# Layer-0 routed feed-forward: weights kept in SBUF for both stages, the sorted token list made by one-hot products, rows gathered and the residual added slot by slot

## The chip, the cores and the metric

The kernel runs on one core of a Trainium2 chip. The metric is device time in microseconds (us) of one launch: the median of several runs for a comparison, and one profiled execution for the reading of the trace. Engines are called by the profile's names: PE (TensorE), DVE (VectorE), ACT (ScalarE), POOL (GpSimd) and SP (SyncE, which only issues transfers).

## The reference, cut to what matters

Twelve stages run one after another on 4096 tokens of 128 numbers (16 x 256). The change concerns the routed feed-forward of layer 0, which runs twice, before and after the layer's attention. Each time the tokens are normalised, sent to one of 8 experts by the largest router logit, and the expert's output is added to the token.

```python
# x: 4096 tokens of DIM = 128, already layer-normed; HIDDEN = 512, E = 8
logits = jnp.einsum('bsd,de->bse', x, router_w) + router_b
top1 = jnp.argmax(jax.nn.softmax(logits, axis=-1), axis=-1)
out = jnp.zeros_like(x)
for i in range(E):
    h = jnp.einsum('bsd,df->bsf', x, w1[i]) + b1[i]          # 128 -> 1024
    a, g = jnp.split(h, 2, axis=-1)
    y = jnp.einsum('bsh,hd->bsd', a * jax.nn.sigmoid(g), w2[i]) + b2[i]
    out = out + jnp.where((top1 == i)[..., None], y, 0.0)
```

## The kernel before, in words

A stage is a block in which each engine has its own instruction stream, written out by hand; engines meet only at semaphores, and at a barrier between stages. `STAGES` lists them: `l0_ffn`, `l0_attn`, `l0_ffn`, and then three stages for each of the layers 1 to 3.

`l0_ffn` has four phases.

1. **Normalise and route.** Eight chunks of four tiles (128 tokens each). DVE writes `xn` (`ln_dve`, L178), PE turns it (L188), ACT keeps it (L194), PE multiplies by the router's weights (L561), DVE adds the bias (L401). POOL makes the scales `rstd` (L159) and copies each chunk of `xn` to `sent` (L368). In the same time SP loads all the stage's weights (L326 to L332: `w1` 4 MB, `w2` 2 MB, the biases spread over the partitions 4.5 MB) and, behind them, writes zeros over the sorted table in DRAM (L337).
2. **Place.** DVE finds each token's row in a list sorted by expert, in which every expert begins on a multiple of 128 (L411 to L469, `pos_i` and `owner_i`). POOL scatters the 32 tiles of normalised rows with their token numbers to `sorted_dram` (L377, 32 indirect transfers); when all have landed, SP loads the table back to `sent` (L342).
3. **Slots.** 40 slots of 128 sorted rows, each with one expert. Per slot: ACT fills `xs` (L515), PE turns it (L580), ACT keeps `xst` (L519), PE makes the two halves `hg` and `ha` (L586, L587), DVE adds the bias (L476, L477), ACT takes the sigmoid (L523), DVE multiplies (L481), PE turns four blocks (L611), ACT keeps `ht` (L547), PE multiplies by `w2` (L594), DVE adds `b2` into `pad` (L486), POOL scatters the result by token number to `sums_dram` (L384). The streams run some slots apart (`run_slots`: body `i` has the first steps of slots `i+1` to `i+3` beside the last ones of `i-1`), and a hardware loop holds two bodies.
4. **Add back.** When all scatters have landed, SP loads `sums_dram` in four pieces (L346), DVE adds each chunk to `x` and takes the new statistics (L505, L201).

## Time and profile before

| | us |
|---|---|
| median of 3 runs | 3355.55 (3349.03 to 3359.73) |
| profiled execution, its own time | 3350.59 |
| span in its trace | 3348.9 |
| PE busy | 2403.8 (72%) |
| DVE busy | 1590.5 (47%) |
| ACT busy | 1083.1 (32%) |
| POOL busy | 849.2 (25%) |
| mean granted TensorE clock | 0.837 of 2.4 GHz |

The span runs from the first to the last instruction; 1.7 us lie around it. The stages follow each other in time, so a stage's own stretch tells what it is worth, and a mean over the span does not. The first `l0_ffn` runs from 13.43 to 271.50 us of the span, the second from 439.40 to 700.79 us. A row of the timeline gives the start, the duration of the merged instructions, engine, line, operation, what is written and read, the count, and in brackets the idle time before it with what ended it.

### The profile page before, as it was taken

What the parts mean: (1) busy time and instruction counts of PE and PEld (TensorE: products, weight loads), DVE (VectorE), ACT (ScalarE), POOL (GpSimd) and SP (SyncE); (2) the same over time, 40 slices, a digit from 0 to 9 for tenths busy, and PEclk for the clock granted to TensorE, in tenths of its full rate; (3) what the DMA queues carried; (4) which work ended last, traced back from release to release, by engine and by line L of the source; (5) the groups of instructions that cost most, each with busy time, mean ns of one, the idle gap of its engine ahead of it and who ended that gap; (6) DMA issues with size and microseconds to landing.
All of it is one profiled execution on the core that took longest, in us unless ns stands there. A gap on an engine that the chain in (4) does not pass through costs nothing. (4 is left out here: it accounts for less than half of the span.)

```text
span 3348.9 us, 45143 instructions
## 1 busy us (share of the span) xinstructions
PE 2403.8 (72%) x13128; PEld 1597.5 (48%) x13129; DVE 1590.5 (47%) x3638; ACT 1083.1 (32%) x2400; POOL 849.2 (25%) x759
## 2 busy tenths in 40 slices
PE   2696945953647361098799971495999879889998
PEld 2463533633635360087466650494444435544554
DVE  3466943675257527933333349634111267761110
ACT  1342312422223121064344431263222135563222
POOL 4323433223611361077100010384000112200000
PEclk9997957985578555599899985697999878999999
DMA  7101062033522356066200013265000043310000
GB/s 202 54 20 30 1 171 59 19 97 84 113 56 77 81 109 182 1 132 136 58 1 1 1 38 92 52 144 138 0 0 0 19 100 78 83 43 26 0 0 25
DMA packets 316644, 211.22 MB, mean 63 GB/s; under 512 B 64711, under 2 KB 300171, under 8 KB 313963
## 3 DMA queue, kind: packets, MB, share of 16 engines
q1 hardware_dynamic: 282731, 177.16, 19.5%
q0 software_dynamic: 33792, 32.57, 5.9%
q8 instruction: 61, 1.00, 0.1%
q14 instruction: 60, 0.49, 0.0%
HBM read 147.94 MB, written 61.12 MB: 62 GB/s over the span
## 5 line engine op out<-in xcount | busy, mean ns | idle before, releaser
L159 POOL TENSOR_TENSOR rstd<-ln_t,power 128x4 f32<-128x4 f32 (+1 forms) x96 | 96.9, 1021 | 636.3 <-DVE ln_t L152 635.9
L2286 DVE TENSOR_TENSOR x<-x,s_y 128x512 f32 (+1 forms) x16 | 11.0, 688 | 496.8 <-PE s_y L2365 496.8
L2350 PE MATMUL s_z<-s_ha,s_wt_h 128*128 128x512 f32 x512 | 222.4, 592 | 0.0
L2357 PE MATMUL s_z<-s_hb,s_wt_h 128*128 128x512 f32 x512 | 222.3, 592 | 0.0
L1897 PE MATMUL s_hu<-s_xgt,s_w 128*128 128x128 f32 x768 | 195.3, 399 | 1.7 <-ACT s_xgt L1837 0.9
L2576 DVE TENSOR_REDUCE s_mx<-s_sa 128x2 f32<-128x512 f32 x256 | 167.1, 685 | 61.3 <-PE s_sa L2729 59.9
L2657 ACT ACTIVATE s_e<-s_sc 128x512 f32<-128x512 f32 x256 | 149.6, 599 | 123.9 <-PE s_sc L2745 122.4
L1897 PEld LDWEIGHTS s_hu<-s_xgt,s_w 128*128 128x128 f32 x768 | 186.7, 327 | 3.0 <-issue 3.0
L188 PE MATMUL s_tp<-ident,xn 128*128 128x128 f32 x352 | 71.5, 339 | 152.1 <-DVE xn L178 148.1
L1883 PE MATMUL s_lp<-ident,s_posf 48*128 48x48 f32 x2 | 0.6, 312 | 233.6 <-DVE s_prob L1765 233.6
L1706 POOL DMA_INDIRECT s_xg<-rows_dram,s_from_i x96 | 95.8, 998 | 269.2 <-DVE s_to_i L1769 240.5
L1718 POOL DMA_INDIRECT acc_dram<-s_yo,s_to_i x96 | 153.4, 1598 | 41.5 <-issue 28.7
L2357 PEld LDWEIGHTS s_z<-s_hb,s_wt_h 128*128 128x128 f32 x512 | 97.3, 190 | 122.5 <-issue 122.5
L2350 PEld LDWEIGHTS s_z<-s_ha,s_wt_h 128*128 128x128 f32 x512 | 96.2, 190 | 115.8 <-issue 115.8
L2729 PE MATMUL s_sa<-s_kx,s_qx 72*128 72x256 bf16 x512 | 112.4, 306 | 36.3 <-DVE s_mx L2576 20.8
L188 PEld LDWEIGHTS s_tp<-ident,xn 128*128 128x128 f32 x352 | 51.1, 175 | 181.7 <-DVE xn L178 137.6
L476 DVE TENSOR_TENSOR s_gb<-s_hg,s_b 128x512 f32<-128x512 f32 x80 | 55.3, 692 | 172.7 <-PE s_ha L587 172.6
L384 POOL DMA_INDIRECT sums_dram<-s_pad,s_sent x80 | 77.7, 972 | 224.7 <-DVE s_pad L486 224.7
L178 DVE TENSOR_SCALAR xn<-x,mean,rstd 128x128 f32 (+1 forms) x352 | 113.5, 424 | 29.0 <-POOL rstd L159 15.4
L194 ACT ACTIVATE xnt<-s_tp 128x512 f32<-128x512 f32 x88 | 52.5, 597 | 210.0 <-PE s_tp L188 202.3
L1102 POOL DMA_INDIRECT acc_dram<-s_yo,s_to_i x64 | 101.5, 1586 | 61.9 <-DMA acc_dram<-s_yo,s_to_i 49.5
L2341 PE MATMUL s_z<-xnt,s_wt_w 128*128 128x512 f32 x256 | 112.7, 593 | 4.6 <-ACT s_wt_w L2300 4.6
(406 smaller groups left out, 5687.6 us busy)
## 6 DMA issues: line engine op xcount, KB each, us to landing
s_w<-in_L_ffn_W_dram SPq DMA_DIRECT2D x96, 256.0 KB
s_kx<-k_dram SPq DMA_DIRECT2D x16, 576.0 KB
s_qx<-q_dram SPq DMA_DIRECT2D x48, 192.0 KB
s_w<-in_L_ffn_w_dram SPq DMA_DIRECT2D x2, 4096.0 KB, 14.4
s_b<-in_L_ffn_b_dram SPq DMA_DIRECT2D x16, 512.0 KB, 7.1
acc_dram<-s_zero SPq DMA_DIRECT2D x16, 512.0 KB, 6.2
acc_dram<-x SPq DMA_DIRECT2D x4, 2048.0 KB, 9.7
x<-acc_dram SPq DMA_DIRECT2D x16, 512.0 KB, 7.0
```

Of the source, the lines that this page charges most:

```text
L159: pool.tensor_tensor(core.rstd[:, tiles], core.ln_t[:, 2, tiles], core.power[:, 0:CT], ALU.pow).then_inc(s.scale_ready.sem, 1)
L178: last = dve.tensor_scalar(core.xn[:, u, j, :], core.x[:, bass.ds(t, 1), :], core.mean[:, bass.ds(t, 1)], core.rstd[:, bass.ds(t, 1)], ALU ...
L188: last = pe.transpose(s.tp[:, u % s.tp_banks, j * P:(j + 1) * P], core.xn[:, u, j, :], core.ident[:, :])
L1102: pool.indirect_dma_start(sums, bass.IndirectOffsetOnAxis(ap=to_i[:, n:n + 1], axis=0), yo[:, n % RING, :], None, compute_op=ALU.add).then ...
L1718: pool.indirect_dma_start(sums, bass.IndirectOffsetOnAxis(ap=to_i[:, n:n + 1], axis=0), yo[:, n % RING, :], None, compute_op=ALU.add).then ...
L1897: last = pe.matmul(hu[:, u, j * P:(j + 1) * P], w1[:, q, :, :].rearrange("p s m -> p (s m)")[:, j::S], xgt[:, u, :], start=True, stop=True)
L2341: pe.matmul(z[:, (2 * f + half) % 4, :], wt[m][:, 0, f * P:(f + 1) * P], core.xnt[:, u, :], start=True, stop=True).then_inc(group_done.sem, 1)
L2350: last = pe.matmul(z[:, o, :], wt["h1"][:, f, o * P:(o + 1) * P], ha[:, f, :], start=f == 0, stop=f == HB - 1)
L2357: last = pe.matmul(z[:, o, :], wt["h2"][:, f, o * P:(o + 1) * P], hb[:, f, :], start=f == 0, stop=f == HB - 1)
L2576: dve.tensor_reduce(mx[:, i, t, 2 * pairs:2 * pairs + 2], sa[:, n % 2, :, :], AX.X, ALU.max).then_inc(max_done.sem, 1)
L2657: act.activation(e[:, n % RING, :, :], sc[:, n % 2, :, :], ACT.Exp).then_inc(exp_done.sem, 1)
L2729: last = pe.matmul(sa[:, n % 2, a, :], qx[0:ROWS, slot, h, t * P:(t + 1) * P], kx[0:ROWS, slot, h, :], start=True, stop=True)
```

## The change

What it does, by part:

- **Weights kept.** `L0Weights` holds router, `w1`, `b1`, `w2`, `b2` and constants over the two `l0_ffn` stages and the attention between them; only the first call loads them. `w2` isn't halved any more: the 0.5 goes into the copy of `ht`. `b2` comes as three bf16 parts in three rows, and one bf16 product per slot adds it on PE.
- **Fields.** `x` becomes part of a row of 136 numbers: the token, its 6 statistics, its scale and its shift. One transfer stores all rows to `x_dram`.
- **List.** Instead of scattering rows, DVE makes one-hot matrices of a token's lane and slot, and 32 small bf16 products on PE sum the token numbers into `ids` (and `to_ids` for the way back). 39 slots take the place of 40.
- **Gather.** For each slot POOL gathers 128 rows of 544 bytes from `x_dram` into `xg`, four slots ahead of the slot whose result it then waits for. ACT normalises while it fills `xs` (scale and bias from the row).
- **Residual and statistics per slot.** DVE adds the result to the row in `xg`, after the next slot's product takes its statistics, and POOL scatters the whole row to `y_dram`. The last phase is one load of `fields` and nothing on DVE.
- The wait for the product of both halves (`h_done`) is split: `g_done` and `g_biased` for the half that the sigmoid needs. The loops of the first phase are written out.

The diff, cut to its core:

```diff
-        self.x = sb("x", [P, TILES, D])
+        self.fields = sb("fields", [P, TILES, D + 8])
+        self.x = self.fields[:, :, 0:D]
+        self.sums = self.fields[:, :, D:D + 6]
+        self.rstd = self.fields[:, :, D + 6]
...
+            sp.wait_ge(nmr_ready.sem, nmr_ready.past(0))
+            sp.dma_start(x_dram[1:TOKENS + 1, :].rearrange("(p t) d -> p t d", p=P), core.fields[:, :, :]).then_inc(x_stored.sem, 16)
...
+            ln_scales_pool(pool, core, s, range(2, CHUNKS))
+            pool.wait_ge(x_stored.sem, 32 if load else 16)
+            pool.wait_ge(ids_ready.sem, 1)
+
+            def gather(i):
+                if i >= 2:
+                    pool.wait_ge(gathered[i % 2].sem, 16 * (i // 2))
+                pool.indirect_dma_start(xg[:, i, :], None, x_dram,
+                                        bass.IndirectOffsetOnAxis(ap=ids[:, i:i + 1], axis=0)).then_inc(gathered[i % 2].sem, 16)
+
+            for i in range(4):
+                gather(i)
+            pool.wait_ge(to_ready.sem, 1)
             for i in range(SLOTS):
+                if i + 4 < SLOTS:
+                    gather(i + 4)
                 pool.wait_ge(y_kept.sem, y_kept.past(i))
...
+                pool.indirect_dma_start(y_dram, bass.IndirectOffsetOnAxis(ap=to_ids[:, i:i + 1], axis=0),
+                                        xg[:, i, :], None).then_inc(stored.sem, 16)
...
+            dve.tensor_tensor(slot_hot[:, :, :], parts[:, 0, :].unsqueeze(2).to_broadcast([P, TILES, SLOTS]),
+                              held.count[:, 0:SLOTS].unsqueeze(1).to_broadcast([P, TILES, SLOTS]),
+                              ALU.is_equal).then_inc(slots_hot.sem, 1)
+            dve.drain()
+            dve.tensor_tensor(slot_id[:, :, 1, :], slot_hot[:, :, :],
+                              held.after[:, :].unsqueeze(2).to_broadcast([P, TILES, SLOTS]), ALU.mult).then_inc(tile_ids.sem, 1)
+            for t in range(TILES):
+                last = dve.tensor_scalar(lane[:, t, :], held.count[:, :], parts[:, 1, t:t + 1], None, ALU.is_equal)
+                if t % CT == CT - 1:
+                    last.then_inc(lane_ready.sem, 1)
+            dve.wait_ge(listed.sem, 1)
+            dve.tensor_copy(id_part[:, :], ha[:, 1, 0:SLOTS])
+            dve.drain()
+            dve.scalar_tensor_tensor(ids[:, :], id_part[:, :], float(TILES), ha[:, 1, SLOTS:2 * SLOTS],
+                                     ALU.mult, ALU.add).then_inc(ids_ready.sem, 1)
...
+                dve.wait_ge(g_done.sem, g_done.past(i))
+                dve.tensor_tensor(gb[:, u, :], hg[:, u, :], b1[:, bass.ds(e, 1), HID:WIDE], ALU.add).then_inc(g_biased.sem, 1)
                 dve.wait_ge(h_done.sem, h_done.past(i))
-                dve.tensor_tensor(gb[:, u, :], hg[:, u, :], b1[:, bass.ds(e, 1), HID:WIDE], ALU.add)
                 dve.tensor_tensor(ab[:, u, :], ha[:, u, :], b1[:, bass.ds(e, 1), 0:HID], ALU.add).then_inc(biased.sem, 1)
...
-            def keep(i):
-                e = dve.value_load(owner_i[0:1, bass.ds(i, 1)], min_val=0, max_val=EXPERTS - 1)
+            def add(i):
                 dve.wait_ge(y_done.sem, y_done.past(i))
-                dve.tensor_tensor(pad[:, bass.ds(i, 1), 0:D], yp[:, 0:P], b2[:, bass.ds(e, 1), :], ALU.add).then_inc(y_kept.sem, 1)
+                xi = xg[:, bass.ds(i, 1), 0:D]
+                dve.tensor_tensor(xi, yp[:, 0:P].unsqueeze(1), xi, ALU.add).then_inc(y_taken.sem, 1)
+
+            def sums(i):
+                dve.drain()
+                dve.bn_stats(xg[:, bass.ds(i, 1), D:D + 6], xg[:, bass.ds(i, 1), 0:D]).then_inc(y_kept.sem, 1)
...
-                    keep(i - 1)
+                    add(i - 1)
                 if after:
                     gate(i + 1, 1 - u)
+                if before:
+                    sums(i - 1)
...
+            def fill_xs(i, u, half, more):
+                act.wait_ge(gathered[u].sem, half * 16 + 16 * (more + 1))
                 act.wait_ge(xt_done.sem, xt_done.past(i - 2))
-                act.activation(xs[:, u, :], sent[:, bass.ds(i, 1), 0:D], ACT.Copy).then_inc(xs_ready.sem, 1)
...
+                act.wait_ge(g_biased.sem, g_biased.past(i))
...
+            for t in range(TILES):
+                if t % CT == 0:
+                    pe.wait_ge(lane_ready.sem, lane_ready.past(t // CT))
+                last = pe.matmul(ha[:, 1, 0:2 * SLOTS], lane[:, t, :], slot_id[:, t, :, :].rearrange("p a n -> p (a n)"),
+                                 start=t == 0, stop=t == TILES - 1)
+            last.then_inc(listed.sem, 1)
...
+                pe.matmul(yp[:, 0:P], held.ones_b[:, :], b2[:, bass.ds(e, 1), :], start=True, stop=False)
                 for f in range(HB):
-                    last = pe.matmul(yp[:, 0:P], ht[:, u, f, :], w2[:, bass.ds(e, 1), f, :], start=f == 0, stop=f == HB - 1)
+                    last = pe.matmul(yp[:, 0:P], ht[:, u, f, :], w2[:, bass.ds(e, 1), f, :], start=False, stop=f == HB - 1)
...
+        with stage(nc) as kept:
+            held = L0Weights(core, kept)
+            l0_ffn(core, held, True)
+            l0_attn(core)
+            l0_ffn(core, held, False)
```

Where the change moves work, the streams are shown as the compiled programs have them (names with `s2_` or `s3_` are the first `l0_ffn`'s; `pool_dma0` is `stored`, `pool_dma1` and `pool_dma2` are `gathered`). POOL's stream from the placing to the end of the first `l0_ffn`, before:

```order
L377 DMA sorted_dram<-s_sent,s_pos_i 5120x129 [waits s2_copied,s2_pos_ready,s2_rows_zeroed]
L377 DMA sorted_dram<-s_sent,s_pos_i 5120x129 x31
L384 DMA sums_dram<-s_pad,s_sent 9216x128 [waits s2_y_kept,s2_sorted_loaded1,s2_sorted_loaded0]
L384 DMA sums_dram<-s_pad,s_sent 9216x128 [waits s2_y_kept] x39
L85 UNCONDITIONAL_BRANCH [waits pool_dma0,pool_dma1]
```

and the same place with the change:

```order
L414 DMA s_xg<-x_dram,s_ids 128x136 [waits pool_dma1]
L414 DMA s_xg<-x_dram,s_ids 128x136 [waits pool_dma2]
L414 DMA s_xg<-x_dram,s_ids 128x136 [waits pool_dma1,s3_to_ready]
L424 DMA y_dram<-s_xg,s_to_ids 9089x136 [waits s3_y_kept]
L414 DMA s_xg<-x_dram,s_ids 128x136 [waits pool_dma2]
L424 DMA y_dram<-s_xg,s_to_ids 9089x136 [waits s3_y_kept]
L414 DMA s_xg<-x_dram,s_ids 128x136 [waits pool_dma1]
L424 DMA y_dram<-s_xg,s_to_ids 9089x136 [waits s3_y_kept]
L414 DMA s_xg<-x_dram,s_ids 128x136 [waits pool_dma2]
L424 DMA y_dram<-s_xg,s_to_ids 9089x136 [waits s3_y_kept]
```

The 32 scatters ahead of the slots are gone, and between the scatters of two slots' results there is now the gather of a later slot, four slots ahead of the result that is waited for next; this goes on to the last gather.

DVE's stream in one slot of the hardware loop, before:

```order
L475 REGISTER_ALU
L476 ISA [waits s2_h_done]
L476 TENSOR_TENSOR s_gb<-s_hg,s_b 128x512
L477 ISA
L477 TENSOR_TENSOR s_ab<-s_ha,s_b 128x512
L484 ISA
L484 TENSOR_LOAD s_owner_i
L484 ISA x2
L486 ISA [waits s2_y_done]
L486 TENSOR_TENSOR s_pad<-s_yp,s_b 128x128
L481 TENSOR_TENSOR s_hs<-s_ab,s_gb 128x512 [waits s2_sig_done]
```

and with the change:

```order
L565 REGISTER_ALU
L566 ISA [waits s3_g_done]
L566 TENSOR_TENSOR s_gb<-s_hg,s_b 128x512
L568 ISA [waits s3_h_done]
L568 TENSOR_TENSOR s_ab<-s_ha,s_b 128x512
L578 ISA [waits s3_y_done]
L578 TENSOR_TENSOR s_xg<-s_yp,s_xg 128x128
L572 REGISTER_ALU [waits s3_sig_done]
L573 TENSOR_TENSOR s_hs<-s_ab,s_gb 128x512 [waits s3_biased]
L582 ISA
L582 BN_STATS s_xg<-s_xg 128x6
```

The bias and the multiplication keep their order; the row's statistics, whose end signals `y_kept` to POOL, stand behind the multiplication that waits for ACT's sigmoid of a later slot, where before the sum of L486, ahead of it, gave that signal.

ACT's stream in two slots behind the hardware loop, with the change (before, the first row of each waited for `xt_done` alone):

```order
L610 ACTIVATE s_xs<-s_xg 128x128 [waits s3_xt_done,pool_dma2]
L615 ACTIVATE s_xst<-s_tp 128x128 [waits s3_xt_done]
L619 ACTIVATE s_gb<-s_gb 128x512 [waits s3_g_biased]
L638 ACTIVATE s_ht<-s_htp 128x512 [waits s3_ht_done]
L610 ACTIVATE s_xs<-s_xg 128x128 [waits s3_xt_done,pool_dma1]
L615 ACTIVATE s_xst<-s_tp 128x128 [waits s3_xt_done]
L619 ACTIVATE s_gb<-s_gb 128x512 [waits s3_g_biased]
L638 ACTIVATE s_ht<-s_htp 128x512 [waits s3_ht_done]
```

Each slot's fill of `xs` now waits for its gather, and the kept transpose, the sigmoid and the kept `ht` of the slots before it stand behind it.

## Rows read from the trace of the kernel before

**Rows 1.** Windows: stretches of the first l0_ffn, busy time by engine, PEclk, DMA share, GB/s.

```profile
61.00:107.00 46.00, 0.00 (x0) 0.00 (x0) 0.00 (x0) 0.16 (x1) 31.00 (x32) 1.00 0.21 64
120.00:245.00 125.00, 120.36 (x622) 80.79 (x621) 79.98 (x147) 54.23 (x145) 36.16 (x37) 1.00 0.06 19
252.00:271.00 19.00, 0.00 (x0) 0.00 (x0) 11.81 (x40) 0.00 (x0) 0.96 (x1) 0.59 0.44 114
```

**Rows 2.** Timeline: first l0_ffn up to its first slot.

```profile
15.76 6.56 DVE L178 TENSOR_SCALAR xn<-x,mean,rstd 128x128 f32<-128x128 f32 x8 [1.14 <-POOL rstd L159]
17.42 4.37 POOL L357 MEMSET s_pad<- 128x5120 f32 x1
...
43.60 0.19 DVE L401 TENSOR_TENSOR s_logits<-s_yp,s_rb 128x32 f32<-128x32 f32 x1 [2.03 <-PE s_yp L561]
...
54.44 0.18 DVE L462 CAST s_pos_i<-s_pos 128x32 uint32<-128x32 f32 x1
...
60.96 1.24 POOL L377 DMA_INDIRECT sorted_dram<-s_sent,s_pos_i  x1 [22.22 <-DMA sorted_dram<-s_pad]
...
100.48 0.96 POOL L377 DMA_INDIRECT sorted_dram<-s_sent,s_pos_i  x1 [0.30 <-issue]
...
106.84 0.51 ACT L515 ACTIVATE s_xs<-s_sent 128x128 f32<-128x128 f32 x2 [54.84 <-DMA s_sent<-sorted_dram]
```

**Rows 3.** Timeline: starts of both l0_ffn stages, and the second one's first slot.

```profile
13.43 0.21 DVE L144 TENSOR_TENSOR ln_t<-sums 128x32 f32<-128x32 f32 x1 [1.22 <-PEq L80]
...
439.40 0.21 DVE L144 TENSOR_TENSOR ln_t<-sums 128x32 f32<-128x32 f32 x1 [1.75 <-PEq L80]
...
535.82 0.51 ACT L515 ACTIVATE s_xs<-s_sent 128x128 f32<-128x128 f32 x2 [55.86 <-DMA s_sent<-sorted_dram]
```

**Rows 4.** Timeline: first result, one slot of the loop, last result, first l0_ffn.

```profile
120.45 0.28 DVE L486 TENSOR_TENSOR s_pad<-s_yp,s_b 128x128 f32<-128x128 f32 x1
...
127.37 0.28 DVE L486 TENSOR_TENSOR s_pad<-s_yp,s_b 128x128 f32 x1
127.48 0.63 ACT L523 ACTIVATE s_gb<-s_gb 128x512 f32<-128x512 f32 x1 [1.67 <-DVE s_ab L477]
...
127.92 0.96 POOL L384 DMA_INDIRECT sums_dram<-s_pad,s_sent  x1 [1.40 <-DVE s_pad L486]
...
128.14 0.69 DVE L481 TENSOR_TENSOR s_hs<-s_ab,s_gb 128x512 f32<-128x512 f32 x1 [0.50 <-ACT s_gb L523]
...
128.50 0.30 ACT L515 ACTIVATE s_xs<-s_sent 128x128 f32 x1
...
128.69 0.27 ACT L519 ACTIVATE s_xst<-s_tp 128x128 f32<-128x128 f32 x1
...
251.47 0.29 DVE L486 TENSOR_TENSOR s_pad<-s_yp,s_b 128x128 f32<-128x128 f32 x1 [2.06 <-PE s_yp L594]
```

**Rows 5.** Line L1706, POOL's 96 gathers of layer 2: their landing.

```profile
DMA to landing us min/median/max: 2.5/2.6/3.5
```

**Rows 6.** Timeline: the attention's normalising on ACT, and one DVE product.

```profile
274.35 1.65 ACT L819 ACTIVATE xn<-x,s_nmr,rstd 128x128 f32<-128x128 f32 x4 [24.32 <-DVE s_nmr L737]
...
326.49 1.35 DVE L760 TENSOR_TENSOR s_prod<-s_cum,s_fk 128x1152 f32<-128x1152 f32 x1
```

**Rows 7.** Tile all_xn (issues, landing) and timeline: first l0_ffn's end, next stage.

```profile
L346 SPq DMA_DIRECT2D all_xn<-sums_dram x4: 360/980/1571, 254.3 to 256.7; - x4
...
DMA to landing us min/median/max: 4.1/6.1/7.0
...
269.98 0.87 DVE L201 BATCH_NORM_STATS2 sums<-x 128x6 f32<-128x128 f32 x4
...
271.50 0.22 DVE L144 TENSOR_TENSOR ln_t<-sums 128x32 f32<-128x32 f32 x1 [0.65 <-PEq L80]
```

**Rows 8.** Windows: a stretch of layer 1's gathered slots, columns as in 1.

```profile
797.00:850.00 53.00, 35.18 (x180) 32.18 (x180) 13.53 (x55) 16.89 (x37) 32.40 (x27) 0.50 0.51 107
```

**Rows 9.** Timeline: the first eight xn of layer 1's routing.

```profile
703.15 2.92 DVE L178 TENSOR_SCALAR xn<-x,mean,rstd 128x128 f32<-128x128 f32 x8 [1.16 <-POOL rstd L159]
```

More of the change, by code:

```diff
@@ L292, in l0_ffn @@
         counted = s.sig("counted")
-        pos_ready = s.sig("pos_ready")
+        slots_hot = s.sig("slots_hot")
+        tile_ids = s.sig("tile_ids")
+        part_ids = s.sig("part_ids")
+        lane_ready = s.sig("lane_ready")
+        listed = s.sig("listed")
+        ids_ready = s.sig("ids_ready")
+        to_ready = s.sig("to_ready")
         owner_ready = s.sig("owner_ready")
-        scattered, stored = s.pool_dmas(core)[0:2]
-        sorted_loaded = [s.sig(f"sorted_loaded{n}") for n in range(2)]
+        stored = s.pool_dmas(core)[0]
+        gathered = s.pool_dmas(core)[1:3]
         xs_ready = s.sig("xs_ready")
@@ L320, in run_slots @@
                     body(pair * 2 + u, u, 2, 3)
[L321 to L322 removed]
+            for i in range(SLOTS // 2 * 2 - 4, SLOTS):
+                body(i, i % 2, 2, min(SLOTS - 1 - i, 3))
         @block.sync
         def _(sp):
[L326 to L327 removed]
@@ L386, in _ @@
+            for u in range(2):
+                pool.wait_ge(gathered[u].sem, 16 * ((SLOTS + 1 - u) // 2))
             pool.wait_ge(stored.sem, 16 * SLOTS)
-            pool.wait_ge(scattered.sem, 16 * TILES)
             s.reset_pool_dmas(pool)
@@ L422, in _ @@
             dve.drain()
[L423 removed]
+            dve.tensor_tensor(hot[:, :, :], hot[:, :, :], by_expert(held.rev, TILES, True), ALU.mult)
             dve.drain()
@@ L494, in body @@
                 if before:
-                    keep(i - 1)
+                    add(i - 1)
                 if after:
                     gate(i + 1, 1 - u)
+                if before:
+                    sums(i - 1)
             run_slots(dve, body)
-            keep(SLOTS - 1)
-            for q in range(4):
-                dve.wait_ge(loaded_back[q].sem, 16)
-                for c in (2 * q, 2 * q + 1):
-                    xc = rows(core.x, c * CT, CT)
-                    dve.tensor_tensor(xc, xc, rows(core.all_xn, c * CT, CT), ALU.add)
-                    dve.drain()
-                    new_sums_dve(dve, core, c)
+            add(SLOTS - 1)
+            sums(SLOTS - 1)
         @block.scalar
         def _(act):
-            each_pair(act, 0, CHUNKS, lambda c, u: ln_act(act, core, s, c, u))
-            def fill_xs(i, u):
+            for c in range(CHUNKS):
+                ln_act(act, core, s, c, c % 2)
+            def fill_xs(i, u, half, more):
+                act.wait_ge(gathered[u].sem, half * 16 + 16 * (more + 1))
                 act.wait_ge(xt_done.sem, xt_done.past(i - 2))
-                act.activation(xs[:, u, :], sent[:, bass.ds(i, 1), 0:D], ACT.Copy).then_inc(xs_ready.sem, 1)
+                one = bass.ds(i, 1)
+                act.activation(xs[:, u, :], xg[:, one, 0:D], ACT.Identity,
+                               bias=xg[:, one, D + 7:D + 8], scale=xg[:, one, D + 6:D + 7]).then_inc(xs_ready.sem, 1)
             def keep_xst(i, u):
@@ L546, in body, with run_act @@
                 act.wait_ge(ht_done.sem, ht_done.past(i))
-                act.activation(ht[:, u, :, :], htp[:, u, :, :], ACT.Copy).then_inc(ht_kept.sem, 1)
-            run_slots(act, body)
+                act.activation(ht[:, u, :, :], htp[:, u, :, :], ACT.Copy, scale=0.5).then_inc(ht_kept.sem, 1)
+            def run_act():
+                for i in range(2):
+                    body(i, i, i, 3, 0)
+                with act.Fori(1, SLOTS // 2 - 2) as pair:
+                    for u in range(2):
+                        body(pair * 2 + u, u, 2, 3, pair)
+                for i in range(SLOTS // 2 * 2 - 4, SLOTS):
+                    body(i, i % 2, 2, min(SLOTS - 1 - i, 3), i // 2)
+            run_act()
         @block.tensor
@@ L552, in _ @@
             ln_pe(pe, core, s, 0, 0)
-            pe.wait_ge(router_loaded.sem, 32)
-            def route(c, u, more=True):
-                if more:
-                    ln_pe(pe, core, s, c + 1, 1 - u)
+            if load:
+                pe.wait_ge(router_loaded.sem, 32)
+            for c in range(CHUNKS):
+                if c + 1 < CHUNKS:
+                    ln_pe(pe, core, s, c + 1, 1 - c % 2)
                 pe.wait_ge(s.xnt_ready.sem, s.xnt_ready.past(c))
```

302 lines of the change are left out of this document (173 added, 129 removed).

## Prediction, made before the changed kernel had run

> **What bounds the kernel now.** I read the windows of the first `l0_ffn`, then the timeline inside each phase, then the landing of POOL's transfers elsewhere in the trace. The stages follow one another, so what counts is where an `l0_ffn` starts and ends: 13.43 to 271.50, and again from 439.40 [rows 3, 7].
>
> Between placing and slots nothing computes: in 61 to 107 PE, DVE and ACT are idle and only POOL works, with 32 scatters [rows 1]. They run from 60.96 to 100.48, one each (100.48 - 60.96) / 31 = 1.27 us, though the positions were ready at 54.44 + 0.18; the first waits for the zeros. The first slot begins at 106.84 [rows 2]. The slots are PE's: 120.36 of 125 us busy [rows 1]. The first result starts at 120.45 and the 40th at 251.47 [rows 4], so 131.0 / 39 = 3.36 us a slot. POOL's scatter of a result is off the path: it starts 0.27 us after the sum ends (127.65 to 127.92) and nobody in the slots waits for it [rows 4]. At the end PE and ACT are idle again, while SP loads and DVE adds [rows 1, 7].
>
> **The change, part by part.**
>
> *Up to the first slot.* The first eight `xn` took 6.56 us beside POOL's 4.37 us clearing of `pad` [rows 2]; the same eight cost 2.92 in a stage without it [rows 9]. The clearing goes, and PE's chain behind them starts 3.3 us earlier (6.56 - 2.92 less what the small constants cost POOL). Last logits: 43.79 - 3.3 = 40.5. Positions come 54.62 - 43.79 = 10.8 later [rows 2]: 51.3. New: three small DVE operations, 0.7 with their drains; two one-hot products of 1248 elements, by the 1152-element product of 1.35 [rows 6] 1.45 each; 32 lane comparisons of 128 elements. The trace has none in bf16; a 128-element DVE operation in a row costs 0.87 / 4 = 0.22 [rows 7] and 2.92 / 8 = 0.37 as `xn` [rows 9]. I take 0.2, nearest the first, so 6.4 (3 to 12). PE's 32 small products run behind them; the last ones and the steps to `ids` add 1.3. Sum: 51.3 + 0.7 + 2.9 + 6.4 + 1.3 = 62.6. POOL starts 0.3 later, and a gather lands 2.6 after its issue (2.5 to 3.5) [rows 5]: first slot at 65.6 instead of 106.84, 41 us gained. In the second stage the distance from its start is the same, 65.6 - 13.43 = 52.2; the slot began at 535.82 - 439.40 = 96.4: 44 us gained [rows 3]. Together **-85**. That no weights are loaded again is in it: they had delayed the zeros that the scatters waited for. In the first stage the store of the rows goes between the weights; both have some 25 us of routing to hide in, and if they were late by all of it the first slot would move by a few us once.
>
> *PE and DVE in a slot.* PE gets one bf16 product, some 0.1 us; one slot fewer saves 3.4 a stage. DVE loses little slack: it is busy 79.98 of 125 [rows 1] and gets 0.22 for the statistics. Neither is the bound, for the next part.
>
> *The ring.* This is the term that decides. POOL's stream is now gather `i+4`, wait for `y_kept` of `i`, scatter `i`, gather `i+5`, ... So gather `b+4` stands behind the scatter of `b-1`. ACT fills `xs` of slot `b+4` in its body `b+1`, and behind that fill, in order, stand the kept transpose, the sigmoid of slot `b+2`. DVE's body `b+1` multiplies with that sigmoid, and only then takes the statistics of slot `b`, whose end is `y_kept(b)`. The ring closes over one slot: `y_kept(b-1)` to `y_kept(b)`. The four slots of lead don't loosen it, since the lead is eaten by three bodies of fill on ACT and one of multiplication ahead of the statistics. Its price:
>
> - `y_kept` to scatter 0.27 [rows 4]; scatter to next issue 1.27 [rows 2]; gather to landing 2.6 [rows 5];
> - fill: with scale and bias from the row, (1.65 for four) [rows 6] about 0.4 to the next instruction, where the plain copy took 128.69 - 128.50 = 0.19 [rows 4]; kept transpose 0.2 to the next; sigmoid 0.63; multiplication 0.03 later, 0.69 [rows 4];
> - drain and statistics 0.36, from the 0.22 a piece [rows 7] and its latency; register instructions between waits and work on ACT and DVE, some 0.15.
>
> Sum 0.27 + 1.27 + 2.6 + 0.4 + 0.2 + 0.63 + 0.72 + 0.36 + 0.15 = 6.6 us. I add 0.2 for turns in which PE has lost its clock (below): **6.8**, against 3.36. The lower end is the shortest landing and no register time, 6.3; the upper is PE at the low clock throughout or a landing of 3.2, 7.4.
>
> The ring holds from `y_kept(0)` to `y_kept(34)`, since gather 38 is the last: 34 turns, 231.2. Before it, from first fill to first statistics, 15.4 (first result at 120.45 - 106.84 = 13.6 [rows 2, 4], then multiplication and statistics). Behind it four free slots, 11.3. Together 257.9, where before there were 251.76 - 106.84 = 144.9 [rows 2, 4]: +113 a stage, **+226** in both.
>
> *The end.* Before, from the last result to the next stage 271.50 - 251.76 = 19.7, of which the last load lands at the latest at 256.7 + 7.0 = 263.7 and DVE adds until 270.85 [rows 7]. Now the scatter, the load and the barrier are left: 2.5 + 2.4 + 7.0 + 0.65 = 12.6. Both stages: **-14**.
>
> The rest of the program is unchanged but for the stride of `x`; I cost it at nothing.
>
> **Sum.** -85 + 226 - 14 = +127. The profiled execution took 3350.59 (span 3348.9 and 1.7 around it), so 3477.6; the median of the runs is 5.0 above the profiled one, so 3482.
>
> The Trainium skill (DMA: Bandwidth & Descriptors, Anatomy of one DMA) gives a POOL transfer about 2.0 us plus its bytes by 436 thousand per us, an estimate of 2.2 for 128 rows of 544 bytes. This case's gathers show 2.5 at the least [rows 5], so the row decides; by the page the ring would be 0.4 shorter and the time some 27 us less, still slower than before.
>
> **Rivals.**
>
> *The gathers are early enough* (faster). If the lead hid them, the slots would stay at PE's pace: -85 - 7 (two slots) - 14 = -106, so 3250. For it speaks that POOL has room: two transfers of 1.27 fit in 3.36. Against it, the order of the streams: even with the least of each row, 0.27 + 1.27 + 2.5 + 0.2 + 0.63 + 0.69 + 0.22 = 5.8, more than a slot. The whole change breaks even at a ring of 6.8 - 127 / 68 = 4.9 us. Chance 0.05.
>
> *PE falls to the low clock and becomes the bound in the slots.* PE works 120.36 / 125 x 3.36 = 3.2 us a slot at the granted clock 1.00 (2.4 GHz) [rows 1] and would be idle half the time in the ring. Where layer 1 works on gathered rows with such gaps, the granted clock is 0.50 (1.2 GHz) [rows 8]. At it a slot costs PE about 6.5, and with its waits up to 7.4; being busy without a gap it should get the high clock back, so it would alternate. At 7.2 to 7.4 throughout: 68 x 0.5 = 34 more, 3516. Chance 0.12.
> The Trainium skill (TensorE: Matmul & The Clock Gate, HAM oscillation) describes a loop that waits for a transfer each turn and starts each turn at the low clock.
>
> *The listing is dear*: 32 comparisons and products at 0.5 instead of 0.2 cost 10 us a stage, and late rows or weights some more: 3505. For it: no row shows these operations. Chance 0.05, and not the sign.
>
> **How the numbers follow.** The ring near 6.8 has 0.76, the other slower ones 0.17, the early gathers 0.05, and 0.02 is for a ring near the break-even. For the range: 6.3 gives 3482 - 34 = 3448, 7.4 gives 3482 + 41 = 3523, and some 8 us for the unknown lanes on either side: 3440 to 3530. A change within 0.3% (10 us) is about what a measurement of this kernel cannot tell. Slower 0.93, within 0.02, faster 0.05.
>
> **What would show it.** In the slots of the changed kernel POOL's scatters stand 6.3 to 7.4 us apart, ACT's fill waits for the gather's DMA each turn, and DVE's multiplication waits for ACT; the first fill is near 66 and at 52 after the second stage's start; `l0_ffn` ends near 336 instead of 271.5. I am wrong if ACT's fill finds its rows landed, if scatters are 3.4 apart, or if PE, at 0.50, is what ACT waits for.

## The result, and the profile after

The changed kernel takes 3488.82 us (median of 4 runs, 3482.75 to 3489.88) where the kernel before takes 3356.09 (4 runs beside it): a ratio of 1.0394, 95% interval 1.0374 to 1.0415, so slower by 3.9%. The forecast was 3482, range 3440 to 3530.

The profiled execution has a span of 3486.8 us against 3348.9, 137.9 more. The two `l0_ffn` stages hold nearly all of it. Timeline of the changed kernel, first statements of the stages and what follows them:

```profile
12.97 0.22 DVE L146 TENSOR_TENSOR ln_t<-fields 128x32 f32<-128x32 f32 x1 [1.29 <-PEq L80]
...
340.88 0.22 DVE L146 TENSOR_TENSOR ln_t<-fields 128x32 f32<-128x32 f32 x1 [11.17 <-PEq L80]
...
509.73 0.22 DVE L146 TENSOR_TENSOR ln_t<-fields 128x32 f32<-128x32 f32 x1 [1.80 <-PEq L80]
...
837.22 0.21 DVE L146 TENSOR_TENSOR ln_t<-fields 128x32 f32<-128x32 f32 x1 [12.30 <-PEq L80]
```

The first stage lasts 327.9 us where it lasted 258.1, the second 327.5 where it lasted 261.4 [rows 3, 7]: 69.8 + 66.1 = 135.9 of the 137.9.

Up to the first slot, timeline of the changed kernel, first stage, and the second stage's first fill:

```profile
15.32 3.56 DVE L180 TENSOR_SCALAR xn<-fields,mean 128x128 f32<-128x128 f32 x8 [1.15 <-POOL fields L161]
...
38.55 0.19 DVE L472 TENSOR_TENSOR s_logits<-s_yp,s_rb 128x32 f32<-128x32 f32 x1 [2.03 <-PE s_yp L663]
...
49.21 0.18 DVE L526 CAST s_pos_i<-s_pos 128x32 int32<-128x32 f32 x1
...
50.08 1.46 DVE L534 TENSOR_TENSOR s_slot_hot<-s_parts,s_count 128x1248 bf16<-128x1248 f32 x1
...
53.01 5.29 DVE L541 TENSOR_SCALAR s_lane<-s_count,s_parts 128x128 bf16<-128x128 bf16 x32
...
59.10 0.20 DVE L547 SCALAR_TENSOR_TENSOR s_ids<-s_id_part,s_ha 128x39 uint32<-128x39 f32 x1
60.20 1.22 POOL L414 DMA_INDIRECT s_xg<-x_dram,s_ids  x1 [35.33 <-DVE s_ids L547]
...
63.03 0.49 ACT L610 ACTIVATE s_xs<-s_xg 128x128 f32<-128x128 f32 x1 [10.07 <-DMA s_xg<-x_dram,s_ids]
...
559.09 0.50 ACT L610 ACTIVATE s_xs<-s_xg 128x128 f32<-128x128 f32 x1 [9.72 <-DMA s_xg<-x_dram,s_ids]
```

The placing phase of 46 us, with its 32 scatters [rows 1, 2], is gone. What stands in its place is 10 us of DVE from 49.2 to 59.3 and one gather's issue and landing. The first slot starts 50.1 us after the stage's start instead of 93.4, in the second stage 49.4 instead of 96.4 [rows 2, 3]: 90.4 us gained in all.

Then the slots take it back, and more. One turn of the loop in the changed kernel's timeline (PE and some of DVE left out where "..." stands):

```profile
188.76 0.29 DVE L582 BATCH_NORM_STATS2 s_xg<-s_xg  x1 [0.19 <-issue]
...
189.34 0.99 POOL L424 DMA_INDIRECT y_dram<-s_xg,s_to_ids  x1 [4.61 <-DVE s_xg L582]
...
190.63 0.97 POOL L414 DMA_INDIRECT s_xg<-x_dram,s_ids  x1 [0.30 <-issue]
...
193.57 0.49 ACT L610 ACTIVATE s_xs<-s_xg 128x128 f32 x1 [5.32 <-DMA s_xg<-x_dram,s_ids]
...
193.97 0.26 ACT L615 ACTIVATE s_xst<-s_tp 128x128 f32<-128x128 f32 x1
194.13 0.62 ACT L619 ACTIVATE s_gb<-s_gb 128x512 f32<-128x512 f32 x1
...
194.87 0.69 DVE L573 TENSOR_TENSOR s_hs<-s_ab,s_gb 128x512 f32<-128x512 f32 x1 [3.06 <-ACT s_gb L619]
...
195.75 0.29 DVE L582 BATCH_NORM_STATS2 s_xg<-s_xg  x1 [0.19 <-issue]
196.32 0.99 POOL L424 DMA_INDIRECT y_dram<-s_xg,s_to_ids  x1 [4.72 <-DVE s_xg L582]
```

Read it as a ring. Each row is released by the one above it, and the last row is the first scatter again, 6.98 us later: statistics end to scatter 0.29, scatter to gather 1.29, gather to fill 2.94, fill 0.40, kept transpose 0.16, sigmoid and its signal 0.74, multiplication 0.69, drain and statistics 0.48. The brackets say the same: POOL idle 4.7 for DVE, DVE idle 3.1 for ACT, ACT idle 5.3 for the DMA. No engine is busy, yet each waits for another. Windows of the loop in both stages (window, its length, then busy us with the number of instructions for PE, PE's weight loads, DVE, ACT and POOL, then the granted clock as a share of 2.4 GHz, the DMA share and GB/s), and its waits (80 to 300 us; engine, what waited, for what: us, times, longest):

```profile
100.00:310.00 210.00, 137.09 (x542) 80.70 (x541) 79.09 (x151) 50.01 (x120) 58.33 (x60) 0.87 0.08 20
600.00:800.00 200.00, 132.71 (x508) 78.22 (x507) 74.69 (x142) 46.81 (x112) 56.85 (x58) 0.84 0.08 20
```

```profile
ACT s_xs L610 <- DMA s_xg<-x_dram,s_ids: 170.7, 32, 6.1
POOL y_dram L424 <- DVE s_xg L582: 146.8, 31, 5.4
DVE s_hs L573 <- ACT s_gb L619: 70.6, 30, 4.1
```

PE was busy 96% of the slots' stretch before [rows 1] and is now busy 65%. The loop's end, timeline of the changed kernel (the scatter of slot 34, the last that a ring turn leads to; then the four free ones, of which the first and the last are shown; then the load back):

```profile
77.31 1.01 POOL L424 DMA_INDIRECT y_dram<-s_xg,s_to_ids  x1 [9.82 <-DVE s_xg L582]
...
316.85 0.99 POOL L424 DMA_INDIRECT y_dram<-s_xg,s_to_ids  x1 [5.11 <-DVE s_xg L582]
322.22 0.98 POOL L424 DMA_INDIRECT y_dram<-s_xg,s_to_ids  x1 [4.39 <-DVE s_xg L582]
...
329.98 0.97 POOL L424 DMA_INDIRECT y_dram<-s_xg,s_to_ids  x1 [1.59 <-DVE s_xg L582]
332.28 2.06 SPq L388 DMA_DIRECT2D fields<-y_dram  x4
```

So 34 turns take 316.85 - 77.31 = 239.5, 7.05 us each, the four free slots 13.1, and from the last statistics to the next stage it is 340.88 - 329.70 = 11.2.

All 68 turns of both stages have this shape. The way from a gather's issue to the fill takes 2.74 to 3.75 us, 3.0 in the mean, and 12 times 3.4 or more; a turn less this way is 4.04 to 4.06 us each time, and 3.86 to 3.87 in the last two turns of a stage. PE's clock does not appear in that figure, though it changes in the loop. Timeline, PE's product for the sigmoid (L696) and the scatters:

```profile
125.70 2.07 PE L696 MATMUL s_hg<-s_w,s_xst 128*128 x2 [0.69 <-issue]
126.67 0.99 POOL L424 DMA_INDIRECT y_dram<-s_xg,s_to_ids  x1 [4.70 <-DVE s_xg L582]
...
132.52 1.12 PE L696 MATMUL s_hg<-s_w,s_xst 128*128 x2 [0.69 <-issue]
133.49 0.99 POOL L424 DMA_INDIRECT y_dram<-s_xg,s_to_ids  x1 [4.55 <-DVE s_xg L582]
...
140.40 0.99 POOL L424 DMA_INDIRECT y_dram<-s_xg,s_to_ids  x1 [4.65 <-DVE s_xg L582]
```

The product's two pieces take 1.12 us at the higher clock and 2.07 at the lower one (1.2 GHz). The turn that holds the slow product lasts 6.82 us, the next one, with the fast product, 6.91.

### The profile page after: what moved, and what is told of

Read it like the earlier page. It is cut to its first block and busy times, and to the rows that moved or that the text cites. A ratio compares the mean times of both kernels' runs of the same rounds, so it can differ in the third digit from the quotient of the medians.

```text
span 3486.8 us, 45187 instructions
## 1 busy us (share of the span) xinstructions
PE 2502.0 (72%) x13236; PEld 1633.8 (47%) x13237; DVE 1610.2 (46%) x3721; ACT 1087.1 (31%) x2387; POOL 844.0 (24%) x746
## 5 line engine op out<-in xcount | busy, mean ns | idle before, releaser
L161 POOL TENSOR_TENSOR fields<-ln_t,power 128x4 f32<-128x4 f32 (+1 forms) x96 | 97.1, 1033 | 635.6 <-DVE ln_t L154 635.3
L2393 DVE TENSOR_TENSOR fields<-fields,s_y 128x512 f32 (+1 forms) x16 | 11.0, 687 | 496.8 <-PE s_y L2472 496.8
L424 POOL DMA_INDIRECT y_dram<-s_xg,s_to_ids x78 | 77.0, 987 | 362.3 <-DVE s_xg L582 362.3
L1825 POOL DMA_INDIRECT acc_dram<-s_yo,s_to_i x96 | 152.8, 1592 | 41.4 <-issue 27.5
L610 ACT ACTIVATE s_xs<-s_xg 128x128 f32 (+1 forms) x78 | 38.6, 495 | 387.1 <-DMA s_xg<-x_dram,s_ids 387.1
L696 PE MATMUL s_hg<-s_w,s_xst 128*128 x156 | 113.0, 814 | 47.1 <-issue 46.9
L573 DVE TENSOR_TENSOR s_hs<-s_ab,s_gb 128x512 f32<-128x512 f32 x78 | 53.9, 692 | 153.8 <-ACT s_gb L619 153.3
L690 PE MATMUL s_tp<-ident,s_xs 128*128 128x128 f32 x78 | 24.5, 314 | 132.0 <-ACT s_xst L615 122.4
```

What stands on the lines that cost most here:

```text
L161: pool.tensor_tensor(core.rstd[:, tiles], core.ln_t[:, 2, tiles], core.power[:, 0:CT], ALU.pow).then_inc(s.scale_ready.sem, 1)
L424: pool.indirect_dma_start(y_dram, bass.IndirectOffsetOnAxis(ap=to_ids[:, i:i + 1], axis=0), xg[:, i, :], None).then_inc(stored.sem, 16)
L696: pe.matmul(hg[:, u, :], xst[:, u, :], w1[:, bass.ds(e, 1), HID:WIDE], start=True, stop=True).then_inc(g_done.sem, 1)
L1825: pool.indirect_dma_start(sums, bass.IndirectOffsetOnAxis(ap=to_i[:, n:n + 1], axis=0), yo[:, n % RING, :], None, compute_op=ALU.add).then ...
```

## The experiments

All kernels are the changed one with a small edit. Ratios are against the kernel before, run on the same chip in the same sitting. A measure that stands beside each time: the mean distance of POOL's 39 scatters in the first stage, last start less first by 38. In the changed kernel it is (330.0 - 77.3) / 38 = 6.65 us (the free slots at the end are in it). A second measure is the length of the two `l0_ffn` stages together in each version's profiled execution. It leaves out the rest of the program, which the edits do not touch and which takes from 2827 to 2843 us in these executions:

| version | both `l0_ffn` stages, us |
|---|---|
| before | 519.5 |
| changed, four slots of lead | 655.4 |
| eight slots of lead | 404.3 |
| five slots of lead | 424.0 |
| scatter behind the gather | 567.8 |
| statistics first | 577.6 |
| PE does more | 664.0 |
| both loosenings | 520.6 |
| eight, weights loaded again | 405.1 |
| eight, without the b2 product | 401.6 |
| eight, early register load | 406.4 |
| eight, both of these | 400.9 |

The theory is the prediction's: the pace is one ring through POOL's in-order queue. The rivals are PE's low clock, or the price of the gathers themselves (POOL's issues and the transfers), which no order of instructions would mend.

**Eight slots of lead.**

```diff
-            for i in range(4):
+            for i in range(8):
                 gather(i)
             pool.wait_ge(to_ready.sem, 1)
             for i in range(SLOTS):
-                if i + 4 < SLOTS:
-                    gather(i + 4)
+                if i + 8 < SLOTS:
+                    gather(i + 8)
```

> POOL issues gather i+8 instead of i+4 ahead of the wait for y_kept of i, in both stages; nothing else changes. Ring theory: the way from y_kept through scatter, gather, fill, sigmoid, product and statistics (7.05 us in the changed kernel) now closes over five slots instead of one, 1.4 us a slot, so PE sets the pace again, near 3.45 us a slot: 3489 - 68 x (7.05 - 3.45) = 3244 us, between 3225 and 3265. Rival, the gathers themselves or PE's low clock set the pace whatever the lead: scatters stay near 7 us apart and the time stays near 3489. Rival, two transfers a slot are too much for POOL: some 5 us a slot, 3350.

Measured: 3241.68 us (4 runs), ratio 0.9674, 95% interval 0.9640 to 0.9708. Summary of L424's scatters, POOL's timeline and the window of the loop in this kernel:

```profile
L424 POOL DMA_INDIRECT y_dram<-s_xg,s_to_ids x39: 967/985/1007, 77.0 to 203.5; - x39
```

```profile
149.31 0.99 POOL L424 DMA_INDIRECT y_dram<-s_xg,s_to_ids  x1 [1.33 <-DVE s_xg L582]
...
152.60 0.98 POOL L424 DMA_INDIRECT y_dram<-s_xg,s_to_ids  x1 [1.03 <-DVE s_xg L582]
```

```profile
100.00:190.00 90.00, 89.01 (x473) 58.39 (x473) 64.62 (x132) 43.82 (x107) 47.89 (x49) 1.00 0.15 39
```

The same instructions, the same transfers, 247 us less. The scatters stand 3.33 us apart, PE is busy 89.0 of 90 us at the granted clock 1.00 (2.4 GHz), and ACT's wait for the gathers is not among the waits any more. So the gathers' price is not what made the changed kernel slow; their place in the queue is. And this version beats the kernel before by 3.3%.

**Five slots of lead**, the same edit with 5 for 8.

```diff
-            for i in range(4):
+            for i in range(5):
...
-                if i + 4 < SLOTS:
-                    gather(i + 4)
+                if i + 5 < SLOTS:
+                    gather(i + 5)
```

> POOL issues gather i+5 ahead of the wait for y_kept of i: one more slot of lead. Ring theory: the same way closes over two slots, 7.05 / 2 = 3.5 us a slot, about PE's own pace; with both limits close, 3.5 to 3.9 a slot: near 3265 us (3250 to 3290). If lead merely hides a fixed share of the landing instead of closing a ring, one slot more of lead would not halve the period, and the time stays above 3400.

Measured: 3260.1 us (2 runs), ratio 0.9729, interval 0.9691 to 0.9767; scatters (214.1 - 77.7) / 38 = 3.59 us apart. One slot more is enough to open most of it: the ring now closes over two slots instead of one. It isn't all hidden, though; the waits between 80 and 260 us still hold this row (against 170.7 us in 32 times in the changed kernel):

```profile
ACT s_xs L610 <- DMA s_xg<-x_dram,s_ids: 47.6, 33, 2.2
```

**The scatter behind the gather.** POOL waits for the statistics of slot i, sends the gather of slot i+5 and only then the scatter of slot i. The issue of the scatter leaves the ring, and nothing else does: the fifth slot of lead is used up by the later place of the gather.

```diff
-            for i in range(4):
+            for i in range(5):
                 gather(i)
...
-                if i + 4 < SLOTS:
-                    gather(i + 4)
                 pool.wait_ge(y_kept.sem, y_kept.past(i))
+                if i + 5 < SLOTS:
+                    gather(i + 5)
                 pool.indirect_dma_start(y_dram, ...)
```

> The same dependence (the gather of slot b+4 still follows y_kept of b-1), but the gather is issued ahead of the scatter of b-1 instead of behind it: the scatter's 1.30 us on POOL leaves the ring. Ring theory: 7.05 - 1.30 = 5.75 us a slot, 68 turns: 3489 - 88 = 3401 us (3385 to 3410); if the gather's landing also waits for the scatter's rows in the queue, some 0.3 a turn less, 3380. If POOL's order is not in the path, the time stays at 3489.

Measured: 3400.58 us (2 runs), ratio 1.0148, interval 1.0109 to 1.0188; scatters 5.47 us apart. 88 us less than the changed kernel is 88 / 68 = 1.3 us a turn, the distance from scatter to next issue (1.27 in [rows 2], 1.29 above); the two stages' own length gives the same, (655.4 - 567.8) / 68 = 1.29. A step's own time came out of the pace, which is what a ring does and what no single busy engine would show.

**The statistics ahead of the next multiplication.** DVE's body takes the statistics of slot i-1 right behind the residual, so that `y_kept` no longer waits for ACT's sigmoid of slot i+1.

```diff
                 if before:
                     add(i - 1)
-                if after:
-                    gate(i + 1, 1 - u)
-                if before:
                     sums(i - 1)
+                if after:
+                    gate(i + 1, 1 - u)
```

> DVE takes a slot's statistics directly behind its addition, ahead of the product that waits for ACT's sigmoid. Ring theory: y_kept of b no longer needs the fill of slot b+4, only that of b+1 does, by way of ht, PE's two halves for another slot and the result: 0.28 + 1.30 + 2.94 + 5.65 (from fill to statistics in the changed kernel's trace) = 10.2 us over two slots, 5.1 a slot: 3489 - 68 x 1.95 = 3356 us (3335 to 3380). If the lead is lost only to the order of the statistics, PE's pace comes back: 3244. If the statistics are not in the path: 3489.

Measured: 3407.29 us (2 runs), ratio 1.0168, interval 1.0132 to 1.0205; scatters 5.55 us apart. The direction is right, the size is not: 82 us less instead of 133, 1.2 us a turn. POOL's timeline of this kernel shows turns in uneven pairs, and the windows are three such pairs, each from scatter to scatter (columns as above; the eighth number is the granted clock):

```profile
147.76 1.17 POOL L424 DMA_INDIRECT y_dram<-s_xg,s_to_ids  x1 [4.62 <-DVE s_xg L582]
...
151.14 0.98 POOL L424 DMA_INDIRECT y_dram<-s_xg,s_to_ids  x1 [0.94 <-DVE s_xg L582]
...
158.03 1.17 POOL L424 DMA_INDIRECT y_dram<-s_xg,s_to_ids  x1 [4.63 <-DVE s_xg L582]
```

```profile
147.76:158.03 10.27, 6.83 (x36) 4.34 (x35) 5.13 (x11) 3.43 (x8) 4.09 (x5) 1.00 0.10 27
180.29:192.12 11.83, 8.61 (x37) 5.04 (x36) 5.13 (x11) 3.54 (x8) 4.10 (x5) 0.86 0.09 24
102.14:115.21 13.07, 9.70 (x37) 6.20 (x36) 5.12 (x11) 3.43 (x8) 4.09 (x4) 0.74 0.08 21
```

Two slots take 158.03 - 147.76 = 10.3 us in the first of them, which is the forecast's 10.2, and so it is in all six pairs of the first stage that PE runs at the granted clock 1.00 throughout: 10.27 to 10.36. The other eleven take 11.8 to 12.0 at 0.86 to 0.87 (12.7 once) and 12.9 to 13.7 at 0.73 to 0.75. So the way was priced rightly and the clock was left out. With the statistics first the ring runs through PE's products, which it did not before, and what PE takes longer at 1.2 GHz now lengthens the turn. The link between clock and pair is read from this trace; no run changed the clock by itself.

**PE does more.** In the changed kernel, four slots of lead, PE makes the sigmoid half's product twice.

```diff
+                pe.matmul(hg[:, u, :], xst[:, u, :], w1[:, bass.ds(e, 1), HID:WIDE], start=True, stop=True)
                 pe.matmul(hg[:, u, :], xst[:, u, :], w1[:, bass.ds(e, 1), HID:WIDE], start=True, stop=True).then_inc(g_done.sem, 1)
```

> The changed kernel with its four slots of lead, and PE makes the product of the sigmoid's half twice in each slot, with the same result. Theory (the ring runs through POOL, the landing, ACT and DVE, and PE only has to be done in time): PE has 7.05 us a slot and uses about 4.5, the extra 0.6 to 0.8 us falls into its idle time; the time stays within 15 us of 3489, and the granted clock rises rather than falls. Rival (PE's low clock and its work set a part of the ring's pace): at least 0.4 us more a turn, 27 us or more, 3516 or above.

Measured: 3503.75 us (4 runs), ratio 1.0445, interval 1.0426 to 1.0465. Scatters and the loop's window:

```profile
L424 POOL DMA_INDIRECT y_dram<-s_xg,s_to_ids x39: 968/985/1007, 80.4 to 335.8; - x39
```

```profile
100.00:310.00 210.00, 157.41 (x600) 87.27 (x600) 79.77 (x150) 49.52 (x120) 58.62 (x60) 0.89 0.08 20
```

PE is 20.3 us busier in 210, and the scatters are 6.72 us apart instead of 6.65 (in the second stage 6.65 instead of 6.63). The time is 15 us longer, at the edge of the theory's bound, but only 8.6 us of it lie in the two stages (664.0 against 655.4), the rest in stages that the edit does not touch and that differ by as much between the other versions. In the first stage 3.1 us arise before the first scatter (80.4 against 77.3), where the pipeline fills and PE is waited for, and 0.07 x 38 = 2.7 us in the turns. Some 0.7 us of PE work a turn costs at most a tenth of itself: PE lies beside the ring, not on it.

**Both loosenings at once**, the edits of the third and fourth run together.

```diff
                 pool.wait_ge(y_kept.sem, y_kept.past(i))
+                if i + 5 < SLOTS:
+                    gather(i + 5)
...
                     add(i - 1)
+                    sums(i - 1)
+                if after:
+                    gate(i + 1, 1 - u)
```

> Four slots of lead, with both loosenings of the ring at once: POOL sends the next gather ahead of the scatter, and DVE takes the statistics ahead of the next slot's multiplication. Alone the first took 88 us off and the second 82, 1.3 and 1.2 us a turn. Theory (the ring is one sum of steps, so what is taken out adds up): 7.05 - 1.3 - 1.2 = 4.55 us a turn, 3489 - 170 = 3319; that is below the break-even of 4.9 us that the prediction gave, so it must be faster than before's 3356. Rival (with one of the steps gone another path is nearly as long, so the second brings little): 3370 to 3400, slower than before.

Measured: 3354.34 us (10 runs), ratio 1.0017, interval 0.9992 to 1.0042; scatters (264.2 - 78.5) / 38 = 4.89 us apart. Neither theory has it: the savings of 88 and 82 us alone make 135 together, not 170, and not 100. What is missing stands in the turns. Timeline of this kernel, one such turn:

```profile
152.59 1.38 POOL L424 DMA_INDIRECT y_dram<-s_xg,s_to_ids  x1 [0.30 <-issue]
...
152.91 2.07 PE L696 MATMUL s_hg<-s_w,s_xst 128*128 x2 [0.69 <-issue]
...
155.13 0.69 DVE L566 TENSOR_TENSOR s_gb<-s_hg,s_b 128x512 f32<-128x512 f32 x1 [2.02 <-PE s_hg L696]
```

The two pieces of the product take 2.07 us, the pace of the lower clock (1.2 GHz), and DVE waits 2.02 us for them. Windows of two pairs of slots, one without such a product and one with it:

```profile
132.69:141.92 9.23, 7.12 (x36) 4.52 (x36) 5.26 (x11) 3.67 (x9) 4.52 (x5) 1.00 0.11 30
152.59:163.30 10.71, 8.65 (x36) 5.04 (x36) 5.10 (x11) 3.51 (x9) 4.50 (x5) 0.84 0.09 26
```

From 91.70 to 244.73 us the five pairs at the granted clock 1.00 take 9.0 to 9.4 us, near the theory's 2 x 4.55 = 9.1, and the ten at 0.84 to 0.85 take 10.5 to 11.2. As in the run with the statistics first, PE is in the ring here, and its low clock is what the sum had left out. That is the prediction's low-clock rival, in a ring where it can bite; it is read from the pairs of one trace and was not tested by itself.

**Are kept weights worth anything?** Eight slots of lead, and the second stage loads its weights again.

```diff
-            l0_ffn(core, held, False)
+            l0_ffn(core, held, True)
```

> Gathers eight slots ahead, and the second stage loads weights, biases and constants again, as the first does. Theory (the weights' loads hide behind the some 50 us of routing, so keeping them is worth nothing by itself): the first stage already shows the price of loading, its first fill 50.1 us after its start against 49.0 in the second; so 1 to 3 us more than with the weights kept, 3244. Rival (keeping the weights is a good part of the 85 us that the front gained): first fill of the second stage 10 us or more later, 3252 or above.

Measured: 3240.33 us (4 runs), ratio 0.9674, interval 0.9656 to 0.9692: no difference from 3241.68. In the trace the second stage's first fill comes 435.04 - 384.9 = 50.1 us after its start instead of 432.20 - 382.8 = 49.4 (the expectation had 49.0), and the stage as a whole is no longer: 202.4 us in both versions. Loading 10.5 MB hides behind the routing. The front's gain is that of the listing, not of the kept weights.

**What bounds the slots at eight slots of lead?** Three runs, each with one engine relieved or both. First PE: without the small product that adds b2.

```diff
-                pe.matmul(yp[:, 0:P], held.ones_b[:, :], b2[:, bass.ds(e, 1), :], start=True, stop=False)
                 for f in range(HB):
-                    last = pe.matmul(yp[:, 0:P], ht[:, u, f, :], w2[:, bass.ds(e, 1), f, :], start=False, stop=f == HB - 1)
+                    last = pe.matmul(yp[:, 0:P], ht[:, u, f, :], w2[:, bass.ds(e, 1), f, :], start=f == 0, stop=f == HB - 1)
```

> Gathers eight slots ahead, and PE's small product that adds b2 is left out (the result lacks b2). In this state PE is busy 89.0 of 90 us, so the product's time comes off the end. Prediction's size of it, 0.1 us: 78 slots x 0.1 = 8 us less than 3242, 3234, and slots 3.3 us apart. Rival (the profile's mean of its row, 0.22 us, is its price): 17 us less, 3225, slots 3.2 apart. Second rival (with the bf16 product gone nothing else is longer, but DVE or ACT takes over as the bound): 3242.

Measured: 3241.98 us (4 runs), ratio 0.9674, interval 0.9658 to 0.9690; scatters 3.31 us apart. That is the second rival's number; of the 8 us that the first size promised, the two stages show 2.7 (401.6 against 404.3). The reason seemed to stand in the waits of the run with eight slots of lead (100 to 190 us):

```profile
DVE s_gb L566 <- issue: 20.2, 26, 0.9
...
DVE s_xg L582 <- issue: 4.9, 26, 0.2
```

DVE's 64.6 us of work and these 25.1 are 89.7 of 90: DVE is as full as PE. So next DVE was relieved, in every second slot, and then both.

```diff
                 if after:
                     gate(i + 1, 1 - u)
+                if after and not u:
+                    kept[0] = expert(i + 2)
                 if before:
                     sums(i - 1)
```

(`expert` is the load of the expert's number into a register; the next `bias` takes it from `kept`.)

> Gathers eight slots ahead, and in every second slot DVE loads the expert's number for the next slot while its multiplication runs, instead of behind the statistics. With gathers eight ahead DVE's 90 us hold 64.6 of work, 20.2 of idle time before the sigmoid half's addition with nothing awaited that the profile shows (26 times, 0.78 each: the register load) and 4.9 before the statistics: 89.7 of 90, as full as PE with 89.0. Theory (both engines are at the end of their time): taking 0.4 us a slot off DVE alone gives at most what PE has free, 1.0 of 90, some 0.04 us a slot: 0 to 3 us, 3239, and the idle time before the addition falls to about 10 us in 90. Rival (DVE alone is the bound, and PE's busy time is partly waiting): 0.2 us a slot or more, 3226 or less.

> As the run with the early register load, and PE's small product that adds b2 is left out too (the result lacks b2). Theory (PE and DVE bound the slots together): now both are relieved, and the pitch falls to PE's 86.35 / 90 x 3.305 = 3.17 us from 3.33, that is 0.15 x 38 turns x 2 stages = 12 us less than 3242, 3230. Rival (a third thing sets the pitch): 3242, slots still 3.3 apart.

Measured: 3241.57 us (4 runs, ratio 0.9646, interval 0.9610 to 0.9682) with the early load, and 3246.03 (4 runs, ratio 0.9666, interval 0.9633 to 0.9700) without the b2 product too; scatters 3.36 and 3.28 us apart. The first row of waits did fall, here in the last of these kernels:

```profile
DVE s_gb L572 <- issue: 8.1, 9, 0.9
```

But the 12 us that the theory of two full engines expected did not come; the two stages show 3.4 of them (400.9 against 404.3). The first of the two runs lies where it was expected, which proves little, since it expected nothing; the second refutes it. PE is then busy 86.5 of 90 and DVE has slack, and the pace is still 3.28. What sets it at that point stays open: the loop has more waits between PE, DVE and ACT than these.

## Why the prediction was right, step by step

The sum was +127 over the profiled execution; the trace has +137.9. By its terms, from the rows above, with the kernel before's 144.9 for the slots and 19.7 for the end in both stages, and for the second stage this summary of its scatters in the changed kernel (its last statistics end at 824.9):

```profile
L424 POOL DMA_INDIRECT y_dram<-s_xg,s_to_ids x39: 971/988/1001, 573.2 to 825.2; - x39
```

The slots take 329.7 - 63.0 = 266.7 and 824.9 - 559.1 = 265.8, the ends 11.2 and 12.3.

| term, both stages | predicted | measured |
|---|---|---|
| up to the first slot | -85 | -90.4 |
| slots, first fill to last statistics | +226 | +242.7 |
| the end | -14 | -16 |

The other stages, costed at nothing, add 2.0. The terms missed by -5, +17 and -2, so part of the miss of the ring was hidden by the better front. The forecast of 3482 also held 5.0 us by which the median of the kernel before lay above its profiled run; the changed kernel's lies 0.3 above. That it came within 7 us of 3489, when the sum was 11 us short, is luck.

*Up to the first slot.* The last logits were forecast for 40.5 and are there at 38.74; the positions follow 10.65 later (10.8 forecast), at 49.4 instead of 51.3. The first eight `xn` gave back 3.0 us (3.56 against 6.56 [rows 2]) where the sum had 3.3 for them, 0.46 comes from an earlier start of the stage, and some 1.6 us I did not follow. The listing was forecast from 51.3 to 62.6 and runs from 49.4 to 59.3; the 32 lane comparisons, for which no row existed, take 5.29 / 32 = 0.165 us each, where I took 0.2 and held up to 0.37 for possible. The rival "the listing is dear" is out by that row. First slot 63.03 instead of 65.6.

*The ring.* This was the term that decides, and the mechanism is shown: rows of one turn release each other as the prediction lists them, and taking out the scatter's issue takes 1.3 us off each of 68 turns. 7.05 us against 6.8. The mis-sized step is the gather's landing, 2.6 in the sum and 2.94 in the turn shown, where layer 2's gathers had a median of 2.6 [rows 5]; over all 68 turns it is 3.0, since 12 of them have 3.4 or more. Drain and statistics are 0.48, not 0.36, and the way from the sigmoid to the product costs 0.12, not 0.03. Against that stand the 0.15 for registers, which the turn shown does not contain, and the 0.2 for turns with PE at its lower clock: such turns exist and are no longer than the others, so that term is worth nothing. That makes 34 x 0.25 x 2 = 17 us, all of what the slots' term lacks. Of the ends, the first fill to the first scatter was over- and the free slots (11.3 forecast, 13.1 measured) under-estimated, by about as much.

The Trainium skill (DMA: Bandwidth & Descriptors, Anatomy of one DMA) would have a gather land after an estimated 2.2 us. This ring's trace shows 2.94, further from it than the rows of before had been, and a ring priced by that page would have been 0.7 us a turn too short.

*The rival that gathers are early enough.* It was given 3250, by leaving the slots at PE's pace. As a forecast for this kernel it was wrong; as a number for what the change is worth without the ring it is close: 3242 with eight slots of lead, 3260 with five.

*The low clock.* In the ring the granted clock is 0.87 and 0.84, so PE does fall to 1.2 GHz in part of the time after it has waited. In the 64 turns whose sigmoid product the timeline holds, the product runs at the higher level in 37 (1.12 us), at the lower in 20 (2.00 to 2.07) and changes within it in 7. Yet a turn less its landing is 4.04 to 4.06 us in all three kinds (but for the last two turns of a stage, above), and more PE work costs next to nothing. The low clock does not set this kernel's pace. Where the ring runs through PE's products, with the statistics first, it costs some 1.5 us or more in a pair of slots. The Trainium skill (TensorE: Matmul & The Clock Gate, HAM oscillation) describes a loop that starts each turn at the low clock; this loop, with PE idle a third of its time, starts its products so in about a third of its turns.

*The break-even* was put at a ring of 4.9 us. The version whose scatters stand 4.89 us apart is as fast as the kernel before, 1.0017 with an interval that spans 1. That figure holds the free slots too, so it agrees a little better than it should; by the totals a turn of the ring in that version is 7.05 - 134.5 / 68 = 5.07.

## What to carry to other kernels

When an in-order queue holds both a load for a later slot and a store that waits for this slot, follow the load forward to the next release of that store and count the slots it comes back over: here four slots of lead were eaten by the three that ACT fills ahead and the one that DVE multiplies ahead, and the gathers' whole latency fell into each slot. A lead is worth only what exceeds the other engines' own run-ahead; one slot more (3260) was worth 229 us, and four more 247. Price such a ring by its turn, step by step, and not by busy shares: with it every engine looks idle, and the cure is an index, not less work. And ask which engines the ring runs through: PE's low clock was free here as long as PE lay beside the ring, and made up nearly all of a missed size once an edit had led the ring through it.
